# Attention and channel-mix kernel: prologue and last group reordered around the second stage

## The reference

```python
# x, ctx: (8, 512, 512); 16 heads of 32; mask: keys of ctx left out
x = x + tanh(g_xattn) * attention(layernorm(x), ctx, ctx, mask, q/k/v/o weights and biases)
h = layernorm(x)
prev = h shifted by one row, with zeros in row 0
xr, xk = mu_r * h + (1 - mu_r) * prev, mu_k * h + (1 - mu_k) * prev
x = x + tanh(g_ffn) * sigmoid(xr @ W_r.T) * (relu(xk @ W_k.T) ** 2 @ W_v.T)
```

## Time and profile before

| | |
|---|---|
| median of 3 runs | 1149.13 us (1148.04 to 1149.97) |
| profiled execution, its own time | 1148.36 us |
| its span in the trace | 1146.6 us |
| PE busy | 1117.5 us, 97% of the span |
| DVE busy | 868.7 us, 76% |
| ACT busy | 684.6 us, 60% |
| POOL busy | 366.3 us, 32% |
| first of 40 slices, PE | 5 tenths busy, all later ones 9 |

### The profile page before, as it was taken

How to read it: one execution, slowest core, us unless ns; L and a number is a source line. 1 busy time by engine, 2 the same in 40 slices (tenths; PEclk the granted TensorE clock), 3 DMA queues, 4 the chain that set the end, 5 groups by cost and what they waited for, 6 DMA issues and landing times.

```text
span 1146.6 us, 21580 instructions
## 1 busy us (share of the span) xinstructions
PE 1117.5 (97%) x7216; PEld 897.7 (78%) x7216; DVE 868.7 (76%) x1964; ACT 684.6 (60%) x1527; POOL 366.3 (32%) x595
## 2 busy tenths in 40 slices
PE   5999999999999999999999999979999999999998
PEld 4778777778778778777877777857888888888887
DVE  6878887888788877887788778868666766666764
ACT  4767776777677777777778767755233322332232
POOL 0143144045036016215203501672443244323421
PEclk9999999999999999999999999989999999999999
DMA  8775675774775577457666457903221113111200
GB/s 271 201 199 148 179 212 140 194 198 134 193 202 151 161 201 208 131 168 217 160 186 194 139 151 204 263 21 102 72 94 56 56 56 109 57 55 55 75 19 37
DMA packets 95709, 162.48 MB, mean 142 GB/s; under 512 B 13296, under 2 KB 22640, under 8 KB 95472
## 3 DMA queue, kind: packets, MB, share of 16 engines
q1 hardware_dynamic: 84912, 143.37, 43.8%
q10 hardware_dynamic: 10688, 17.73, 5.4%
HBM read 109.91 MB, written 49.57 MB: 139 GB/s over the span
## 4 chain that ended last, share of the span: by engine, by line
PE 91%; DVE 2%; DMA 2%; POOL 1%; issue 1%; ACT 0%; SPq 0%; DVEq 0%; ACTq 0%; POOLq 0%
PE bank L562 30%; PE bank L631 18%; PE bank L593 14%; PE bank L622 10%; PE bank L643 9%; PE bank L601 8%; PE bank L756 1%; DMA w_raw<-wvvT 1%; DVE neg_s L1089 1%; DMA rden_dram<-ctx_sb 0%; POOL w2r_lo L1442 0%; POOL w2v_lo L1442 0%; PE bank L608 0%; PE bank L745 0%; DMA qk_dram<-k_lo 0%
## 5 line engine op out<-in xcount | busy, mean ns | idle before, releaser
L914 ACT ACTIVATE probs<-neg_s,negmax 128x512 f32<-128x512 f32 x512 | 367.9, 720 | 64.1 <-DVE negmax L1089 61.9
L1089 DVE CUSTOM_DVE_ANT_0 neg_s<-bank,mask_big 128x512 f32<-128x512 f32 x512 | 343.8, 679 | 9.6 <-DVE mask_big L1149 1.0
L631 PE MATMUL bank<-ident,probs 128*128 128x128 f32 x2048 | 308.0, 273 | 3.0 <-DVE pT L1095 3.0
L631 PEld LDWEIGHTS bank<-ident,probs 128*128 128x128 f32 x2048 | 248.4, 141 | 51.4 <-issue 6.3
L1095 DVE COPY pT<-bank 128x512 f32<-128x512 f32 x254 | 174.9, 688 | 110.3 <-PE bank L631 108.8
L622 PE MATMUL bank<-k_stack,q_stack 96*128 96x512 f32 x512 | 242.2, 474 | 0.0
L921 ACT COPY pT<-bank 128x512 f32<-128x512 f32 x258 | 149.7, 580 | 128.2 <-PE bank L631 127.4
L643 PE MATMUL bank<-pT,v_sb 128*32 128x512 f32 x1024 | 116.5, 595 | 0.6
L993 ACT ACTIVATE relu<-bank 128x512 f32<-128x512 f32 x32 | 19.1, 598 | 143.3 <-PE bank L562 141.3
L622 PEld LDWEIGHTS bank<-k_stack,q_stack 96*128 96x128 f32 x512 | 97.5, 190 | 1.1
L1429 POOL TENSOR_TENSOR o_sb<-o_sb,w_raw 128x1024 f32<-128x1024 f32 x15 | 36.6, 2442 | 189.6 <-DVE o_sb L1304 189.6
(11 more groups left out here) (158 smaller groups left out, 2140.8 us busy)
## 6 DMA issues: line engine op xcount, KB each, us to landing
k_stack<-qk_dram SPq DMA_DIRECT2D x93, 256.0 KB, 5.3
q_stack<-qk_dram SPq DMA_DIRECT2D x93, 256.0 KB, 5.8
cT_raw<-ctxT SPq DMA_DIRECT2D x8, 1024.0 KB, 7.9
rden_bc<-rden_dram SPq DMA_DIRECT2D x128, 64.0 KB, 6.0
ctx_dram<-ctx_sb SPq DMA_DIRECT2D x32, 256.0 KB, 2.2
c_raw<-ctx_dram SPq DMA_DIRECT2D x16, 512.0 KB, 4.1
x_in<-x SPq DMA_DIRECT2D x16, 512.0 KB, 5.0
qk_dram<-k_hi SPq DMA_DIRECT2D x31, 256.0 KB, 2.7
```

The lines of the kernel that those rows point to most:

```text
L631: mm = nc.tensor.transpose(pt_bank[i % 2][:, a * P:(a + 1) * P], probs[:, i % P_RING, a * P:(a + 1) * P], ident[:])
L914: nc.scalar.activation(probs[:, i % P_RING, :], neg_s[:, i % SM_RING, :], ACT.Exp, bias=negmax[:, k:k + 1], scale=-1.0, accum_out=den[:, g ...
L1089: nc.vector.tensor_tensor_reduce(neg_s[:, i % SM_RING, :], s_bank[tile_no(b, c, i) % S_BANKS][:], mask_big[:, q, :], 1.0, 3e38, ALU.add, A ...
```

## The change

Prologue. The load of the identity matrix is issued ahead of those of wk and the first context. In ACT's program the cut of wq moves behind the high part of K 0, next to that of wv. PE makes all of K 1 ahead of Q 0, the first term of Q 1 ahead of the last of Q 0, and V 0 by a new function `first_values`, whose term with wv's low part comes last in each half, and whose first half waits for that part only before that term. ACT's copies of Q 0 begin when its high part is there, and only the third band waits for the low part. On DVE the mask comes ahead of Q 0's low part, the statistics of batch 1's first two tiles come ahead of the first scores, the third mask step ahead of V 0, and the scaling of the bias (`gate_bias`) goes after tile 1 of group 1. The other two statistics come after tiles 5 and 9 (before: 5 and 7, behind two after 1 and 3), the store of mean and root after tile 14 (before 12), and batch 1's first turned x after tiles 1 and 2 of group 1 (before: tiles 0 and 2 of group 0), behind the spread, which stays after tile 0 of group 1.

Last group. W2 3 is loaded into the buffer of W2 0, once POOL has cut that, and is issued in group 1 of batch 7 (before: into the buffer of W2 1, in group 2); `x1` lies in the buffer of W2 1. POOL's order becomes: W2 0, context 0, W2 1, bias 0, W2 3, bias 1, root, then a wait for the normalised rows, context 1, then a wait for the first mix, W2 2.

```diff
--- before.py
+++ after.py
@@ -78,8 +78,8 @@
 
     first, then = nb - 2, nb - 1
     if nb == 1:
-        return {(0, 0, 0): ("xT", 0), (0, 0, 2): ("xT", 1), (0, 0, 12): ("store", 0), (0, 1, 0): ("spread", 0),
-                (0, 1, 14): ("xT", 2), (0, 2, 0): ("xT", 3)}
+        return {(0, 0, 14): ("store", 0), (0, 1, 0): ("spread", 0), (0, 1, 1): ("xT", 0), (0, 1, 2): ("xT", 1),
+                (0, 1, 15): ("xT", 2), (0, 2, 0): ("xT", 3)}
     return {(first, 3, 0): ("rows", 0), (first, 3, 2): ("rows", 1), (first, 3, 10): ("rows", 2),
             (first, 3, 12): ("rows", 3), (first, 3, 14): ("xT", 0), (then, 0, 3): ("xT", 1), (then, 0, 10): ("store", 0),
             (then, 0, 14): ("spread", 0), (then, 1, 10): ("xT", 2), (then, 1, 12): ("xT", 3)}
@@ -87,7 +87,7 @@
 
 def stats_at(nb):
 
-    return ((0, 0, 1), (0, 0, 3), (0, 0, 5), (0, 0, 7)) if nb == 1 else (
+    return (None, None, (0, 0, 5), (0, 0, 9)) if nb == 1 else (
         (nb - 2, 3, 7), (nb - 2, 3, 9), (nb - 1, 0, 3), (nb - 1, 0, 5))
 
 
@@ -206,7 +206,7 @@
         w2_raw = halves("w2_raw", CH, D)
         x_in = halves("x_in", UM, D)
 
-        x1 = [w2_raw[0][:, h * UM:(h + 1) * UM, :] for h in range(2)]
+        x1 = [w2_raw[1][:, h * UM:(h + 1) * UM, :] for h in range(2)]
         xh = sb(stage2, "xh", [P, UM, D])
         xT_first = sb(stage2, "xT_first", [P, CH, 1 + UNIT])
         diff = sb(stage2, "diff", [P, CH, UNIT])
@@ -351,9 +351,9 @@
 
             for t in range(TT):
                 load_x(t)
+            sp.dma_start(ident[:], ident_d).then_inc(ident_ld, 16)
             load_w(1, wk)
             load_ctx(0)
-            sp.dma_start(ident[:], ident_d).then_inc(ident_ld, 16)
             for t, a in ((bq_col, bq), (bk_col, bk)):
                 sp.dma_start(t[:], a).then_inc(bias_ld, 16)
             load_w(0, wq)
@@ -428,8 +428,8 @@
 
             def load_w2(n):
                 if n == 3:
-                    sp.wait_ge(w2_lo_done[1], 1)
-                sp.dma_start(w2_raw[n % 2][:], W2[n].rearrange("(a p) e -> p a e", p=P)).then_inc(w2_ld[n % 2], 16)
+                    sp.wait_ge(w2_lo_done[0], 1)
+                sp.dma_start(w2_raw[n % 3][:], W2[n].rearrange("(a p) e -> p a e", p=P)).then_inc(w2_ld[n % 3], 16)
 
             def store_context(b, c):
                 sp.wait_ge(ctx_done, b * GROUPS + c + 1)
@@ -481,8 +481,8 @@
                     if c == 1 and not more:
                         load_turned(0, 0)
                         load_turned(0, 1)
+                        load_w2(3)
                     if c == 2 and not more:
-                        load_w2(3)
                         load_w2r()
                     if g:
                         store_context(*previous)
@@ -655,6 +655,18 @@
                                           start=start and a == 0, stop=stop and a == CH - 1)
                 return mm
 
+            def first_values(keys):
+
+                for act_part, w in ((act_hi, w1_hi), (act_lo, w1_hi), (act_hi, w1_lo)):
+                    if w is w1_lo:
+                        pe.wait_ge(w_lo_done, 3)
+                    for a in range(CH):
+                        mm = nc.tensor.matmul(first_v_bank[:, keys * UNIT:(keys + 1) * UNIT],
+                                              act_part[1][:, a, keys * P:(keys + 1) * P], w[2][:, a, 0:UNIT],
+                                              start=act_part is act_hi and w is w1_hi and a == 0,
+                                              stop=w is w1_lo and a == CH - 1)
+                return mm
+
             def chunk_rounded(a):
                 pe.wait_ge(side_hi, hi_no(None, ("C", a)) + 1)
 
@@ -670,26 +682,27 @@
             product(1, 0, k_first, w1_lo, act_hi)
             product(1, 0, k_first, w1_hi, act_lo, stop=True, ready=chunk_split).then_inc(side_mm, 1)
 
+            product(1, 1, second_bank[1], w1_hi, act_hi, start=True)
+            product(1, 1, second_bank[1], w1_lo, act_hi)
+            product(1, 1, second_bank[1], w1_hi, act_lo, stop=True).then_inc(second_mm[1], 1)
+
             pe.wait_ge(w_hi_done, 2)
             pe.wait_ge(side_hi, hi_no(None, ("T", TT - 1)) + 1)
             product(0, 0, q_first, w1_hi, act_hi, start=True)
             pe.wait_ge(side_done, done(side_no(None, ("T", TT - 1))))
             product(0, 0, q_first, w1_hi, act_lo)
-            product(1, 1, second_bank[1], w1_hi, act_hi, start=True)
-            product(1, 1, second_bank[1], w1_lo, act_hi)
+            pe.wait_ge(side_done, done(side_no(None, ("K", 0))))
+            product(0, 1, second_bank[0], w1_hi, act_hi, start=True)
             pe.wait_ge(w_lo_done, 2)
             product(0, 0, q_first, w1_lo, act_hi, stop=True).then_inc(side_mm, 1)
-            product(1, 1, second_bank[1], w1_hi, act_lo, stop=True).then_inc(second_mm[1], 1)
-
-            pe.wait_ge(side_done, done(side_no(None, ("K", 0))))
-            product(0, 1, second_bank[0], w1_hi, act_hi, start=True)
             product(0, 1, second_bank[0], w1_hi, act_lo)
             product(0, 1, second_bank[0], w1_lo, act_hi, stop=True).then_inc(second_mm[0], 1)
-            pe.wait_ge(w_lo_done, 3)
-            side(None, "V", 0, 0, 2)
+
+            pe.wait_ge(w_hi_done, 3)
+            first_values(0)
             for i in range(AHEAD_S):
                 scores(0, 0, i)
-            side(None, "V", 0, 1, 2)
+            first_values(1).then_inc(side_mm, 1)
             scores(0, 0, AHEAD_S)
 
             def batch(b):
@@ -860,6 +873,8 @@
 
             def copy_queries(j):
                 for band, source in enumerate((qk_hi, qk_hi, qk_lo)):
+                    if j == 0 and band == 2:
+                        act.wait_ge(side_done, done(side_no(None, ("Q", 0))))
                     act.dma_start(stack[0][0][HD * band:HD * (band + 1), j, :].bitcast(F32),
                                   source[0][HD * j:HD * (j + 1), :].bitcast(F32)).then_inc(copied[0][j], 16)
 
@@ -925,12 +940,12 @@
                 if kind == "K":
                     act.wait_ge(bias_ld, 16 * 2)
                     nc.scalar.mul(bq_neg[:], bq_col[:], -SCALE).then_inc(consts, 1)
+                if (kind, n) == ("Q", 0):
                     split_w(0)
-                if (kind, n) == ("Q", 0):
                     split_w(2)
                     act.wait_ge(consts, 1)
                 side(None, kind, n)
-            act.wait_ge(side_done, done(side_no(None, ("Q", 0))))
+            act.wait_ge(side_hi, hi_no(None, ("Q", 0)) + 1)
             for j in range(2):
                 copy_queries(j)
             act.wait_ge(small_ld, 16 * 5)
@@ -1142,19 +1157,23 @@
                 side(None, "T", n)
             side(None, "K", 0)
             split_w(0)
+            dve.wait_ge(mask_ld, 16)
+            nc.vector.tensor_scalar(mask_big[:], mask_u8, MASKED, None, ALU.mult).then_inc(mask_done, 1)
             dve.wait_ge(consts, 1)
             side(None, "Q", 0)
             split_w(2)
-            dve.wait_ge(mask_ld, 16)
-            nc.vector.tensor_scalar(mask_big[:], mask_u8, MASKED, None, ALU.mult).then_inc(mask_done, 1)
+            for t in range(2):
+                row_stats(1, t)
             dve.wait_ge(mask_done, 1)
             mask_and_min(0, 0, 0)
             mask_and_min(0, 0, 1)
+            mask_and_min(0, 0, 2)
             dve.wait_ge(bv_ld, 16)
             side(None, "V", 0)
-            mask_and_min(0, 0, 2)
-            dve.wait_ge(consts, 2)
-            nc.vector.tensor_scalar(tgbo[:], tgbo[:], tg[:, 0:1], None, ALU.mult).then_inc(consts, 1)
+
+            def gate_bias():
+                dve.wait_ge(consts, 2)
+                nc.vector.tensor_scalar(tgbo[:], tgbo[:], tg[:, 0:1], None, ALU.mult).then_inc(consts, 1)
 
             def tile_step(b, c, i):
                 if not (is_last(b) and c == GROUPS - 1 and i + AHEAD_S >= TILES):
@@ -1170,6 +1189,8 @@
                 for c in range(GROUPS):
                     for i in range(TILES):
                         tile_step(b, c, i)
+                        if (b, c, i) == (0, 1, 1):
+                            gate_bias()
                         if i == TILES - 2:
                             reciprocals(b, c)
                         if b + c and i == DIVIDE_STEP:
@@ -1197,7 +1218,7 @@
                 if (c, i) in LAST_RESIDUAL:
                     m = LAST_RESIDUAL.index((c, i))
                     if m == 0:
-                        dve.wait_ge(w2_lo_done[0], 1)
+                        dve.wait_ge(w2_lo_done[1], 1)
                         dve.wait_ge(xb_done, 1)
                         dve.wait_ge(consts, 3)
                     residual(0, 0, m, o_bank[1 - m])
@@ -1429,11 +1450,11 @@
                 nc.gpsimd.tensor_tensor(o_sb[:, h], o_sb[:, h], x1[h], ALU.add).then_inc(o_done, 1)
 
             def split_w2(n):
-                raw = w2r_raw if n == 2 else w2_raw[n % 2]
+                raw = w2r_raw if n == 2 else w2_raw[n % 3]
                 if n == 2:
                     pool.wait_ge(w2r_ld, 16)
```

(10 more changed lines are left out.)

## The result

| | before | after |
|---|---|---|
| median | 1149.03 us (1148.04 to 1149.97, 4 runs) | 1137.97 us (1136.75 to 1139.26, 4 runs) |
| profiled execution, its own time | 1148.36 us | 1139.26 us |
| its span | 1146.6 us | 1137.5 us |

The ratio is 0.9905, with a 95% interval of 0.9891 to 0.9919. Forecast were 1137.5 us as the time and 11.2 us as the gain; the medians differ by 11.1 us. The execution that was profiled is the slowest of the four and shows 9.1 us. That difference is the larger part of what there is to learn here. Times here are compared between executions in the fast state only; one of the four of run e5, at 3979.00 us, was in the slow one and is left out.

What follows compares the result with a forecast made beforehand. PE, busy for 97% of the span, bounds the kernel, so only its idle time can be given back: 1148.36 - 1.65 - 2.2 - 7.35 = 1137.2 us, predicted as 1137.5; range for 8 in 10, 1134.5 to 1142.5 us.

Steps and rivals of the forecast that it cites:

- The start: Prologue up to the first turned tile: that tile comes 1.65 us sooner, with bounds of 0.7 and 3.3 us.
- a wait of 1.15 us for wv's low part: Prologue, last term of V 0: PE idle for about 1 us, a new wait that sets nothing.
- The price of 0.2 us on the context: Prologue: the 64 KB matrix now ahead of the context's load costs that load some 0.2 us.
- Group 0: Group 0 on DVE and PE: PE's stalls shrink, 2.2 us won in all, with 1.0 and 3.0 us as ends.
- Batch 1's x: POOL, batch 1's x: later by at most some 2 us against PE, costed at nothing; without cover 2 us.
- Where stage 2 begins: Last group into stage 2: POOL's root comes sooner, 7.65 us won on PE, 7.35 us net.
- The new wait: Before O 2 where stage 2 begins: PE waits 2.1 us for context 1 on POOL.
- The 0.3 us that I took off for `mix_k_lo`: Stage 2: W2 2's cut beside DVE's `mix_k_lo` costs 0 to 1.2 us on DVE, taken as 0.3 on PE.
- The bound of one piece: Stage 2, by the skill's rule: `mix_k_lo` waits for at most one of POOL's pieces, 1.25 us.
- rival 4: Stage 2: W2 2's cut ends after PE wants it, slower than before, 1150 us or more; chance 0.02.
- The sum: Whole kernel: 1148.36 - 1.65 - 2.2 - 7.35 = 1137.2 us on the profiled execution, predicted as 1137.5 us.
- Rival 1: Before O 2: the clock falls in PE's wait, costing 2.5 to 5 us, so 1140 to 1142.5; chance 0.15.

Runs made afterwards that it cites:

- e5: The changed kernel with Q 1's stores ahead of K 1's reload and context 1 ahead of the root in POOL's list; 1136.75 us, ratio to before 0.9894.
- e7: The kernel before with only the identity matrix's load moved ahead of wk and the context; 1148.07 us, ratio to before 0.9997.
- e8: e3 with Q 1's high and low parts made after tile 2 in place of tile 3; 1138.04 us, ratio to before 0.9909.
- e0: The changed kernel run again without an edit; 1137.79 us, ratio to before 0.9903.
- e1: The changed kernel's prologue and group 0 alone, with the last group and POOL's list as before; 1145.72 us, ratio to before 0.9968.
- e3: The changed kernel with both stores of Q 1 issued ahead of the reload of K 1's bands; 1136.70 us, ratio to before 0.9892.
- e6: The changed kernel without POOL's wait for the first mix ahead of W2 2's cut; 1139.39 us, ratio to before 0.9914.
- e11: The changed kernel with W2 3 loaded as before and x1 in W2 0's buffer, POOL's list in the changed order; 1140.96 us, ratio to before 0.9935.
- e2: The kernel before with only W2 3's load, x1's buffer and POOL's list changed; 1142.22 us, ratio to before 0.9941.
- e10: The changed kernel with context 1's rounding made twice on POOL, for a longer wait; 1140.16 us, ratio to before 0.9929.
- e9: e8 with context 1 ahead of the root in POOL's list as well; 1136.57 us, ratio to before 0.9897.
- e4: The changed kernel with context 1 ahead of the root in POOL's list; 1137.54 us, ratio to before 0.9902.

## Why the prediction was right, step by step

**The start.** Forecast 1.65 us at the first turned tile, measured 1.83 and 1.78 against the span's start. That two profiles agree so well is in part luck: over the eleven with the changed prologue that tile starts at 30.68 to 32.10, for 33.60 and 33.68 with the whole prologue of before. The single steps hold to 0.6 us: transposes at 10.78 (forecast 10.3; x had landed 0.3 us later in that execution), Q 0's high part at 24.24 (24.75), its third copy at 26.34 (26.95), scores at 28.84 (29.15), and a wait of 1.15 us for wv's low part that sets nothing (about 1). The price of 0.2 us on the context can't be seen: it landed at 12.83, sooner than the 13.34 of the earlier trace rows, but over the profiles with the matrix ahead it landed anywhere from 12.20 to 13.58. e7 shows that the matrix alone does not carry the gain.

**Group 0.** This step failed. Forecast 2.2 us; measured a loss of 0.7 us in one profile and a gain of 1.3 in the other. DVE's part was right: the stalls for pT in group 0 fell from 2.6 us to 0.4, and in the profile without a wait for q_stack (e8) group 0 took 20.0 us, 2.5 less than before. The wait comes on top one for one: in the nine profiles with the changed prologue and a clock of 1.00 throughout it (e0, e1, e3, e5, e6, e8 to e11), group 0 less its wait for q_stack is 20.0 to 20.3 us. What I left out is the round trip of Q 1 and K 1 through DRAM: store, landing, reload. The prediction does not name it, so its cost stood at nothing. The trace of the kernel before shows how little room it had (SP's issue of the reload, and PE's score of tile 16):

```profile
45.98 1.38 SPq L411 DMA_DIRECT2D q_stack<-qk_dram  x3
```

```profile
51.44 0.48 PE L622 MATMUL bank<-k_stack,q_stack 96*128 96x512 f32 x1
```

The score starts 5.46 us after the reload is issued. In the eight profiles in which PE waited for it with SP's queue in this order, the score started 5.3 to 5.7 us after the issue. So before the change the reload was just in time, and in e2, where it was issued at 47.44, it was late. The change moved the user from 51.44 to 47.2, by 4.2 us, and the issue of the reload by only 2.6 us in the first profile (43.38) and 3.2 us in e0 (42.76); the differences, 1.6 and 1.0 us, are the waits of 1.5 and 1.1. The price is 0.2 to 1.5 us of waiting, and in the first profile 1.7 us more for the half clock behind it. There the score that waited started at 48.69, and a turned tile's four matmuls took 1.05 us at 49.59 for the 0.60 of others:

```profile
50.00:51.00 1.00, 1.00 (x6) 0.90 (x5) 0.00 (x0) 0.32 (x1) 0.00 (x0) 0.50 1.03 397
```

**Batch 1's x.** Forecast: at most 2 us later on POOL against PE, at no cost. Measured: its first piece 8.5 us later in absolute time, its last at about the same time as before, so some 1 us later against PE, which was 1.15 us ahead; at no cost in the two profiles of the changed kernel and at 2.2 us in e8's. The 8.7 us to landing were not foreseen. POOL's later waits cover them in the changed kernel, but did not in e8.

**Where stage 2 begins.** Forecast 7.65 us on PE before the price on `mix_k_lo`, measured 7.66 (40.58 less 32.92). The load of W2 3 was issued at 718.55, for 733.96 before, and POOL did not wait for it. X 0 came 8.57 us sooner, less the 1.35 us by which the stretch began sooner: 7.22 for 7.25. The new wait was 1.76 us for 2.1; the forecast's own terms (756.95, 1.04, 2.73 and 0.2 off) end at 760.5 and not at the 760.7 written there, so 0.2 of that was a slip in the sum. The 0.3 us that I took off for `mix_k_lo` were to show at the second unit, behind the last mark, and that rest of the span has the same length in all three columns of the table. `mix_k_lo` took 1.45 us in place of 1.23, and w2r_lo's four pieces 6.01 in place of 4.99, so POOL bore most of the meeting and not DVE. DVE met a piece of POOL's near its end, and POOL's next piece, at 771.79, lasted 2.26 us for the 1.28 of the others, to the end of DVE's operation. That POOL waited for it agrees with the section "Who interferes with whom" of "SBUF — State Buffer" in the Trainium skill, by which the one that comes second waits. The bound of one piece, 1.25 us, was kept. W2 2's cut ended at 775.3, 4.6 us ahead of its use, so rival 4 did not come near. e6 shows the same for the operations that the added wait protects.

**The sum** came out at 11.1 us for 11.2, and part of that is luck. By e0's profile group 0 gave 0.9 us less than forecast (1.3 for 2.2), since the failing step costs about 1 us there, and the start and the last stretch gave 0.4 us more together (1.8 for 1.65, 7.64 for 7.35): errors of opposite sign. Rival 1, the clock's fall in the wait for context 1, is rare at 1.7 to 1.8 us (in none of the profiles of after, e0, e2, e3, e8 and e11, in e6's); at 2.8 us it came in e10's profile and, by the mean clock, in all its executions.

**A faster version.** e3 is the best candidate: 1136.70 us, 1.1 us under the changed one in the same series, with the lowest ratio of all, though the intervals overlap and only a part of the gain is explained. e9 has the lowest median, 1136.57 us, but the ratio is no lower (0.9897), and it carries e8's risk.

## What to carry to other kernels

When a change makes an engine's work sooner, list every transfer whose result that work uses, and write its slack beside it before counting a gain: the one without slack takes the gain back. The slack can be read from the trace of before: the time from a transfer's issue to its first use, beside the time that it takes to land. A load that is moved later to free an issue slot may land much later than it was moved, if it falls among large reloads. A new short wait on PE is cheap only while it stays short; 1 us more cost 2.8 us in e10's profile.

## What the runs showed of the hardware

The granted clock fell to 0.50 behind a wait for q_stack of 1.48 us in group 0 of the first profile of the changed kernel. Behind the wait of 1.7 to 1.8 us in the last group it stayed at 1.00 in six profiles and fell in one (e6), for which no run gives a reason; behind 2.8 us it fell in e10's profile, and the mean clock of 0.998 in all its executions speaks for the same there. In one execution it was granted at 0.95 for some 170 us from the start (e4), where the kernel's other three executions had a mean of 0.998 to 1.000, which made the stretch to batch 7 2.1 us longer. Three issues of one reload on SP's queue took 2.60 us in e0 and 1.27 in the execution profiled first. A load of 256 KB took 2.9 us from issue to landing early in group 0 of the kernel before, and 8.7 us in the changed kernel beside the reloads of group 2.
